# Attention's softmax denominators from GpSimd's sums of three probability chunks, both parts in one accumulation, and two passes over the early weights moved to ScalarE

## The chip, the cores and the metric

The kernel runs on one core of a Trainium2 chip. Times are device microseconds of one execution. TensorE (PE) multiplies, VectorE (DVE) and ScalarE (ACT) read its results, GpSimd (POOL) works on SBUF only, and SyncE (SP) issues most DMAs. Engines run their own instruction lists in order and meet at semaphores.

## The reference, cut to what matters

A cross-attention with two softmaxes (496 context rows, and 16 "dca" rows with their own keys and values) is followed by a mixture-of-experts layer. Only the attention matters here: for each of 4 x 16 = 64 heads (HD = 32, 512 queries),

```python
def _attn(q, k, v):
    s = jnp.einsum('bhqd,bhkd->bhqk', q, k) * SCALE
    p = jax.nn.softmax(s, axis=-1)
    return jnp.einsum('bhqk,bhkd->bhqd', p, v)
ctx = _attn(qT, k, v)                      # 496 main keys
ctx_dca = _attn(qT, k_dca, v_dca)          # 16 dca keys
ctx = ctx + DCA_WEIGHT * ctx_dca
return ctx @ Wo + bo
```

## The kernel before, in words

The program runs in stages: projections, attention (`attend`), output projection with routing, and the experts in two passes. The change is in `attend`, apart from a small constant table.

Attention walks over 64 heads with a software pipeline. A step `u` of the loop has two slots (`p` = 0 and 1). In step `u` PE makes the scores of head `u` in the layout queries x keys (`scores`, tile `a_psS`, two matmuls in each slot); DVE takes the negated row maxima from them (L866 over the 496 main keys, L867 over the 16 dca keys). The maxima are turned by small matmuls (`max_rows`, `a_psM`, in slot 0 only), ACT copies them as two more rows behind the queries (L822), and for head `u - 2` PE makes the scores again, transposed and with the maximum subtracted (`scores_t`, `a_psT`, one chunk of 128 keys in each matmul, four chunks to a head). ACT exponentiates each chunk into the tiles P0 to P3 (`p_t`, L807); chunk 3 holds the last main keys and the dca keys.

Four heads make a group, and there are 16 groups. With a lag of six steps, the P chunks of a group are multiplied in pieces that PE takes one or two at a time in the eight slots `h` = 0 to 7 of four steps (`chunk`). A piece (`four`) is four matmuls, one per head, each into its own 32 partitions; in float32 the trace shows it as eight. There were ten pieces to a group: four for the main denominators (P0 to P3 against columns of ones, `a_psD`), four for the values (`a_psO`), one for the dca values (`a_psOd`) and one for the dca denominators (`a_psD` again). The order in every slot is: T (an `a_psT` matmul), two S (`a_psS`), T, then the slot's piece or pieces, and M (the four `a_psM` matmuls) where `p` is 0. `a_psS` is one pair of banks: the S of a slot wait until DVE has read those of the slot before. `a_psT` is two banks: a T waits for the exponential two before it.

DVE turns and inverts the denominators between its reductions (L830, L833, L836 for the main part, L846, L849, L853 for dca) and multiplies (L841, L856). POOL adds both parts (`o_sum`, L790), ACT rounds the sum to float16 (the "hi" half, L813), and POOL subtracts that to get the "lo" half (L794).

Beside this, 12 half matrices of expert weights are prepared during attention, one for each four steps: SP loads one into `a_raw` once the one before is split, and POOL makes its float16 half (L167), scales it in place (L172, with a tiny L171 ahead) and subtracts (L175).

Of the kernel before, what the change touches and what calls it, by code (L numbers as in the profile page):

```python
# [82 lines left out]
def build(nc, t, out, upto=99, dbg=None):  # L83
# [17 lines left out]
    with ctx:  # L101
# [57 lines left out]
        def split_half(pool, raw, loaded, arrived, k, half, m, n, piece):  # L159
# [32 lines left out]
def project(nc, t, sem, g_):  # L192
# [51 lines left out]
    with ExitStack() as ps:  # L244
# [80 lines left out]
        def _(pool):  # L325
# [12 lines left out]
            pool.memset(ones[:, 0, :], 1.0).then_inc(s["masks"], 1)  # L338
# [152 lines left out]
        def _(dve):  # L491
# [118 lines left out]
            dve.tensor_copy(ones[:, 1, :], m_main[:, :].broadcast_to([P, HD]))  # L610
            dve.tensor_copy(ones[:, 2, :], m_dca[:, :].broadcast_to([P, HD]))
# [85 lines left out]
def attend(nc, t, sem, g_):  # L697
# [7 lines left out]
    RING = (6, 7, 7, 8)  # L705
# [9 lines left out]
    d_t = sb("d_t", [P, S], F32)  # L715
    d_rec = sb("d_rec", [P, S // HD, 1], F32)
# [4 lines left out]
    names = """sel max m_mm mrow s_mm t_mm exp d_mm v_mm dca_mm d_seen dd_seen d_rec dd_rec rec_main rec_dca o_main o_dca o_sum o_hi o_lo"""  # L721
# [4 lines left out]
    with ExitStack() as ps:  # L726
# [45 lines left out]
        def _(pool):  # L772
# [11 lines left out]

            for u in range(LAST):
                gr, h = group(u, 0)
                if there(gr - 1) and h == 4:
                    pool.wait_ge(s["o_main"], gr)
                    pool.wait_ge(s["o_dca"], gr)
                    pool.tensor_tensor(o_sum[:, :], o_sum[:, :], r_dca[:, :], ALU.add).then_inc(s["o_sum"], 1)  # L790
                if there(gr - 1) and h == 6:
# [4 lines left out]
                if n is not None and j < 3:  # L796
                    m, k, half = early[n]
                    g_["split_half"](pool, raw[:, :, :], raw_ld, n + 1, k, half, m, n, j)

        @block.scalar  # L800
        def _(act):
            def exps(w, k):

                act.wait_ge(s["t_mm"], TB * w + k + 1)
                if w >= RING[k]:
                    act.wait_ge(s["v_mm"], TB * ((w - RING[k]) // G) + k + 1)
                act.activation(probs(w, k), psT[:, k % 2], ACT.Exp, scale=SCALE / (QS * QS)).then_inc(s["exp"], 1)  # L807
# [7 lines left out]
            for u in range(LAST):  # L815
                for p in range(2):
# [6 lines left out]
                    hi_part(*group(u, p))  # L823

        @block.vector
        def _(dve):
            def main_part(gr, h):
                if there(gr) and h == 4:
                    dve.wait_ge(s["d_mm"], gr + 1)
                    dve.transpose(d_t[:, :], psD[:, :]).then_inc(s["d_seen"], 1)  # L830
                if there(gr) and h == 5:
                    dve.wait_ge(s["d_seen"], gr + 1)
                    dve.reciprocal(d_rec[:, :, :], d_t[:, :].rearrange("p (a o) -> p a o", o=HD)[:, :, 0:1]).then_inc(s["d_rec"], 1)  # L833
                if there(gr) and h == 6:
# [955 lines left out]
```

## Time and profile before

| | |
|---|---|
| time, median of 3 runs (lowest to highest) | 1215.59 us (1213.75 to 1219.01) |
| the profiled execution's own time | 1215.54 us |
| its span | 1213.4 us |
| PE busy over the span | 1050.7 us, 87% |
| DVE, ACT, POOL busy | 631.5, 491.9, 558.6 us |
| `p_t` exponentials on ACT (L807) | 256 of 595 ns |
| maxima on DVE (L866) | 128 of 1194 ns |
| matmuls into `a_psD`, `a_psO` (L900) | 640 of 607 ns, 512 of 601 ns |

Busy time counts the matmul records with their overlaps merged; since matmuls are pipelined, the distance between the starts of two of them tells what one costs, not its duration. Attention lies between about 190 and 512 us of the span.

### The profile page before, as it was taken

How to read it: one execution, taken by the hardware profiler on the slowest of the kernel's cores; microseconds unless marked ns; L12 is line 12 of the kernel's file. 1: busy time of each engine (PE TensorE's matmuls, PEld its weight loads, DVE VectorE, ACT ScalarE, POOL GpSimd, SP SyncE). 2: the span in 40 equal slices, each digit the busy share in tenths (PEclk: the TensorE clock that was granted, in tenths of full speed). 3: DMA queues.
4: the chain of work that ended last, by engine and by line, in shares of the span. 5: the costliest groups of instructions: out<-in, count | busy, mean ns of one | idle time of the engine just before them, and what ended most of it. 6: DMA issues, size and time to landing. Idle time of an engine off the chain costs nothing. (4 is left out here: it accounts for less than half of the span.)

```text
span 1213.4 us, 18924 instructions
## 1 busy us (share of the span) xinstructions
PE 1050.7 (87%) x5825; PEld 478.9 (39%) x5826; DVE 631.5 (52%) x1123; ACT 491.9 (41%) x886; POOL 558.6 (46%) x505
## 2 busy tenths in 40 slices
PE   2789955999999999689439999999999999967896
PEld 1445431222222222145315545445545455523453
DVE  6777744677777777445543333233333322215644
ACT  2466553566666666323213333333333333312231
POOL 1365551143434421232337799898999800032111
PEclk9889985899999999889759999999999999989899
DMA  6144451222122211045136434333434311146244
GB/s 233 40 116 127 135 143 52 58 77 76 61 80 62 76 62 42 19 160 180 72 119 245 165 124 137 121 121 121 138 122 137 104 52 52 35 146 228 87 122 139
DMA packets 88074, 133.02 MB, mean 110 GB/s; under 512 B 7992, under 2 KB 46904, under 8 KB 88016
## 3 DMA queue, kind: packets, MB, share of 16 engines
q1 hardware_dynamic: 75040, 90.55, 23.5%
q0 software_dynamic: 11648, 40.38, 9.8%
q10 hardware_dynamic: 1328, 1.36, 0.4%
q8 instruction: 32, 0.52, 0.2%
q14 instruction: 26, 0.21, 0.1%
HBM read 85.60 MB, written 46.66 MB: 109 GB/s over the span
## 5 line engine op out<-in xcount | busy, mean ns | idle before, releaser
L866 DVE TENSOR_REDUCE nm<-a_psS 128x2 bf16<-128x992 f32 x128 | 152.8, 1194 | 83.9 <-PE a_psS L877 83.9
L807 ACT ACTIVATE p_t<-a_psT 128x512 f32<-128x512 f32 x256 | 145.6, 595 | 62.9 <-PE a_psT L893 59.0
L1706 PE MATMUL e_psU<-w_exp,e_xT 128*128 (+1 forms) x528 | 130.8, 384 | 11.4 <-issue 8.0
L1706 PE MATMUL e_psY<-w_exp,e_gT 128*128 (+1 forms) x528 | 128.1, 379 | 2.7 <-issue 1.7
L1706 PE MATMUL e_psG<-w_exp,e_uT 128*128 (+1 forms) x528 | 128.4, 379 | 2.2 <-DVE e_uT L1658 2.2
L893 PE MATMUL a_psT<-q_stk,k_stk 98*128 98x512 f16 x256 | 101.6, 402 | 0.4 <-ACT p_t L807 0.4
L877 PE MATMUL a_psS<-k_stk,q_stk 96*128 96x512 f16 x256 | 82.3, 405 | 21.9 <-DMA k_stk<-k_dram 14.5
L1687 DVE TENSOR_TENSOR e_g<-e_g,e_u 128x512 f32<-128x512 f32 x44 | 51.6, 1172 | 91.6 <-ACT e_g L1623 91.6
L175 POOL TENSOR_TENSOR w_exp<-e_raw,w_exp 128x1024 f32 (+1 forms) x42 | 90.8, 2161 | 6.0 <-POOL e_raw L172 4.5
L1658 DVE TENSOR_TENSOR e_gT<-e_psGT,e_gT 128x512 f16<-128x512 f32 x44 | 30.4, 692 | 108.0 <-ACT e_gT L1596 108.0
L900 PE MATMUL a_psD<-p_t,ones 128*32 128x512 f32 x640 | 85.1, 607 | 0.0
L167 POOL TENSOR_TENSOR w_exp<-e_raw,ws_tile 128x1024 f32 (+1 forms) x42 | 80.6, 1920 | 4.3 <-DMA e_raw<-in_L_ffn_Wup_dram 3.5
L1706 PEld LDWEIGHTS e_psU<-w_exp,e_xT 128*128 128x128 f16 x528 | 49.2, 99 | 84.1 <-issue 31.7
L1603 ACT ACTIVATE e_u<-e_psU 128x512 f32<-128x512 f32 x44 | 26.3, 597 | 119.1 <-PE e_psU L1706 119.1
L1706 PEld LDWEIGHTS e_psG<-w_exp,e_uT 128*128 128x128 f16 x528 | 50.6, 98 | 55.2 <-DVE e_uT L1658 2.5
L1706 PEld LDWEIGHTS e_psY<-w_exp,e_gT 128*128 128x128 f16 x528 | 50.7, 98 | 48.3 <-issue 5.2
L790 POOL TENSOR_TENSOR o_sum<-o_sum,r_dca 128x512 f32<-128x512 f32 x16 | 20.4, 1275 | 106.2 <-DVE r_dca L856 106.2
L900 PE MATMUL a_psO<-p_t,v_all 128*32 128x512 f32 x512 | 67.4, 601 | 0.0
L1623 ACT ACTIVATE e_g<-e_psG 128x512 f32<-128x512 f32 x44 | 26.3, 597 | 93.5 <-PE e_psG L1706 93.5
L822 ACT ACTIVATE q_stk<-a_psM 2x512 f16<-2x512 f32 x64 | 37.4, 585 | 65.7 <-PE a_psM L884 65.6
L167 POOL TENSOR_TENSOR w_exp<-a_raw,ws_tile 128x1024 f16<-128x1024 f32 x12 | 22.7, 1893 | 87.2 <-DMA a_raw<-in_L_ffn_Wsu_dram 45.9
L1658 DVE TENSOR_TENSOR e_xT<-e_psX,e_xT 128x512 f16<-128x512 f32 x44 | 30.4, 692 | 52.7 <-ACT e_xT L1596 52.7
(315 smaller groups left out, 1875.1 us busy)
## 6 DMA issues: line engine op xcount, KB each, us to landing
e_x<-xs_dram SPq DMA_DIRECT2D x38, 256.0 KB, 2.8
ys_dram<-e_y SPq DMA_DIRECT2D x38, 256.0 KB, 2.0
q_dram<-q_st SPq DMA_DIRECT2D x24, 256.0 KB, 2.8
k_dram<-k_st SPq DMA_DIRECT2D x24, 256.0 KB, 3.6
q_stk<-q_dram SPq DMA_DIRECT2D x64, 96.0 KB
k_stk<-k_dram SPq DMA_DIRECT2D x64, 96.0 KB
e_raw<-in_L_ffn_Wup_dram POOLq DMA_DIRECT2D x12, 512.0 KB, 4.2
e_raw<-in_L_ffn_Wgate_dram POOLq DMA_DIRECT2D x12, 512.0 KB, 4.2
```

The costliest lines, as they stand in the source:

```text
L167: pool.tensor_tensor(hi, w, ws, ALU.mult).then_inc(w_scaled, 1)
L175: pool.tensor_tensor(lo, w, hi, ALU.subtract).then_inc(split_done, 1)
L807: act.activation(probs(w, k), psT[:, k % 2], ACT.Exp, scale=SCALE / (QS * QS)).then_inc(s["exp"], 1)
L822: act.activation(q_stk[K3:KR, (u - 1) % SLOTS, :], psM[0:2, :], ACT.Copy, scale=1.0 / QS).then_inc(s["mrow"], 1)
L866: dve.tensor_reduce(pair[:, :, 0:1].rearrange("p q o -> p (q o)"), psS[:, :, 0:NMAIN], AX.X, ALU.max, negate=True)
L877: ins = pe.matmul(psS[:, i], q_stk[0:K3, u % SLOTS, q * P:(q + 1) * P], k_stk[0:K3, u % SLOTS, :], start=True, stop=True)
L893: pe.matmul(psT[:, k % 2], k_stk[0:KR, w % SLOTS, k * P:(k + 1) * P], q_stk[0:KR, w % SLOTS, :], start=True, stop=True).then_inc(s["t_mm"], 1)
L900: ins = pe.matmul(dst[j * HD:(j + 1) * HD, :], stationary(n), probs(n, k), start=first, stop=last, tile_position=(0, j * HD))
L1603: act.activation(u[:, j], psU[:, :], ACT.Copy, scale=1.0 / WS).then_inc(s["u_r"], 1)
L1658: return dve.tensor_tensor(pair[:, 1], src[:, :].rearrange("p (k n) -> p k n", n=P), pair[:, 0], ALU.subtract)
L1687: dve.tensor_tensor(g[:, :], g[:, :], u[:, j], ALU.mult).then_inc(s["g_r"], 1)
L1706: ins = pe.matmul(dst[:, :], stationary, moving, start=(k == 0 and chunks[0] == 0), stop=(k == len(terms) - 1 and chunks[-1] == KD - 1))
```

## The change

- The main denominators use POOL's sum of P0, P1 and P2 of each head (`p_sums`, a ring of six tiles `p_sum`), so two pieces are left for them: the sums against ones, and P3 against ones masked to the main keys.
- The denominator matrix has 32 columns of which the first half belongs to the main part and the second half to dca; P3 against it gives both, so the dca denominators need no piece of their own. A group has seven pieces. Slot 7 has none.
- DVE turns the denominators once, inverts two columns of each block, and spreads each of them. The dca spread and the main product stand together in slot 7, the dca product in slot 0 of the next group.
- ACT makes the float16 half and the scale pass of the early weights; POOL keeps the subtraction. The hi half of the attention output moves on ACT from `h` 4 to `h` 3; on POOL the sum moves from `h` 4 to `h` 2 and the lo half from 6 to 4.
- The rings of P chunks are smaller (5, 5, 6, 7 tiles for 6, 7, 7, 8).

PE around slots 2 to 5 of a group: ahead of a slot's piece stand T, S, S, T. `a_psD` are denominators, `a_psO` values; `p_t_2080` to `p_t_2083` are P0 to P3 before. Before:

```order
L900 MATMUL a_psD<-p_t_2082,ones 32x512 x4
L884 MATMUL a_psM<-ident_b,nm 2x128 x4
L893 MATMUL a_psT<-q_stk,k_stk 128x512
L877 MATMUL a_psS<-k_stk,q_stk 128x512 x2
L893 MATMUL a_psT<-q_stk,k_stk 128x512
L900 MATMUL a_psD<-p_t_2083,ones 32x512 x4
L900 MATMUL a_psO<-p_t_2080,v_all 32x512 x4
L893 MATMUL a_psT<-q_stk,k_stk 128x512
```

And now (`p_t_2084` is P3, `p_sum` the sum of the three others):

```order
L931 MATMUL a_psD<-p_sum,ones 32x512 x4
L915 MATMUL a_psM<-ident_b,nm 2x128 x4
L924 MATMUL a_psT<-q_stk,k_stk 128x512
L908 MATMUL a_psS<-k_stk,q_stk 128x512 x2
L924 MATMUL a_psT<-q_stk,k_stk 128x512
L931 MATMUL a_psD<-p_t_2084,ones 32x512 x4
L924 MATMUL a_psT<-q_stk,k_stk 128x512
```

Slot 3 has lost its second piece; slot 6 has lost one in the same way, and slot 7 its only one.

POOL over one group before: the early weights' passes (L167 to L175) and two operations of the output.

```order
L790 TENSOR_TENSOR o_sum<-o_sum,r_dca 128x512
L167 TENSOR_TENSOR w_exp<-a_raw,ws_tile 128x1024
L794 TENSOR_TENSOR oT_all<-o_sum,oT_all 128x512
L171 TENSOR_TENSOR seen<-ws_tile 128x1
L172 TENSOR_SCALAR a_raw<-a_raw 128x1024
L175 TENSOR_TENSOR w_exp<-a_raw,w_exp 128x1024
```

And now, from the step with slots 0 and 1 on:

```order
L802 TENSOR_TENSOR p_sum<-p_t_2081,p_t_2082 128x512
L805 TENSOR_TENSOR p_sum<-p_sum,p_t_2083 128x512
L175 TENSOR_TENSOR w_exp<-a_raw,w_exp 128x1024
L802 TENSOR_TENSOR p_sum<-p_t_2081,p_t_2082 128x512
L805 TENSOR_TENSOR p_sum<-p_sum,p_t_2083 128x512
L814 TENSOR_TENSOR o_sum<-o_sum,r_dca 128x512
L802 TENSOR_TENSOR p_sum<-p_t_2081,p_t_2082 128x512
L805 TENSOR_TENSOR p_sum<-p_sum,p_t_2083 128x512
L818 TENSOR_TENSOR oT_all<-o_sum,oT_all 128x512
```

The sum of the output (L814) now stands behind both additions of a head's P chunks.

ACT at the hi half of the output, before:

```order
L807 ACTIVATE p_t_2081<-a_psT 128x512
L822 ACTIVATE q_stk<-a_psM 2x512
L813 ACTIVATE oT_all<-o_sum 128x512
L807 ACTIVATE p_t_2082<-a_psT 128x512
L807 ACTIVATE p_t_2083<-a_psT 128x512
```

And now:

```order
L850 ACTIVATE q_stk<-a_psM 2x512
L835 ACTIVATE p_t_2083<-a_psT 128x512
L835 ACTIVATE p_t_2084<-a_psT 128x512
L841 ACTIVATE oT_all<-o_sum 128x512
L835 ACTIVATE p_t_2081<-a_psT 128x512
L835 ACTIVATE p_t_2082<-a_psT 128x512
```

The hi half moved from the middle of a step to the end of the step before, between the exponentials of two heads.

The diff, cut to its core:

```diff
-    RING = (6, 7, 7, 8)
+    RING = (5, 5, 6, 7)
+    SUMS = 6
...
+        def scale_half(act, raw, loaded, arrived, k, half, m, n, piece):
+            hi = w_exp[:, k % E * 2 + half, m, 0, :, :]
+            if piece == 0:
+                act.wait_ge(loaded, 16 * arrived)
+                act.activation(hi, raw, ACT.Copy, scale=WS).then_inc(w_scaled, 1)
+            else:
+                act.wait_ge(w_scaled, 2 * n + 1)
+                act.activation(raw, raw, ACT.Copy, scale=WS).then_inc(w_scaled, 1)
...
+            def p_sums(w):
+                at_least(pool, s["sums_mm"], (w - SUMS) // G + 1)
+                t_ = p_sum[:, w % SUMS, :]
+                pool.wait_ge(s["exp"], TB * w + 2)
+                pool.tensor_tensor(t_, probs(w, 0), probs(w, 1), ALU.add).then_inc(s["sum_1"], 1)
+                pool.wait_ge(s["exp"], TB * w + 3)
+                pool.wait_ge(s["sum_1"], w + 1)
+                pool.tensor_tensor(t_, t_, probs(w, 2), ALU.add).then_inc(s["sum_2"], 1)
+
             for u in range(LAST):
                 gr, h = group(u, 0)
-                if there(gr - 1) and h == 4:
+                if head(u - 2):
+                    p_sums(u - 2)
+                if there(gr - 1) and h == 2:
                     pool.wait_ge(s["o_main"], gr)
                     pool.wait_ge(s["o_dca"], gr)
                     pool.tensor_tensor(o_sum[:, :], o_sum[:, :], r_dca[:, :], ALU.add).then_inc(s["o_sum"], 1)
...
             def hi_part(gr, h):
-                if there(gr - 1) and h == 4:
+                if there(gr - 1) and h == 3:
                     act.wait_ge(s["o_sum"], gr)
...
+                n, j = early_at(u)
+                if n is not None and j < 2:
+                    m, k, half = early[n]
+                    g_["scale_half"](act, raw[:, :, :], raw_ld, n + 1, k, half, m, n, j)
...
+                if there(gr) and h == 7:
+                    at_least(dve, s["o_sum"], gr)
+                    dve.transpose(blocks(r_dca[:, :]), spread(1)).then_inc(s["rec_dca"], 1)
+                    dve.wait_ge(s["v_mm"], TB * (gr + 1))
+                    dve.wait_ge(s["rec_main"], gr + 1)
+                    at_least(dve, s["o_lo"], gr)
+                    dve.tensor_tensor(o_sum[:, :], psO[:, :], r_main[:, :], ALU.mult).then_inc(s["o_main"], 1)
...
             def chunk(gr, h):
-                if h < TB:
-                    denominator(gr, h)
-                if TB - 1 <= h < 2 * TB - 2:
-                    values(gr, h - TB + 1)
-                if h == 2 * TB - 2:
+                if h in (0, 1):
+                    values(gr, h)
+                if h in (2, 3):
+                    if h == 3:
+                        pe.wait_ge(s["exp"], TB * (gr * G + G))
+                    denominators(gr, h == 3)
+                if h in (4, 5):
+                    values(gr, h - 2)
+                if h == 6:
                     dca(gr)
-                if h == 2 * TB - 1:
-                    values(gr, TB - 1)
```

## Rows read from the trace of the kernel before

**Rows 1.** Busy time by engine in one stretch of attention, with PE's granted clock.

```profile
340.00:380.00 40.00, 40.00 (x280) 11.57 (x273) 30.90 (x52) 25.22 (x45) 15.82 (x13) 1.00 0.23 73
```

**Rows 2.** Timeline of PE, slots 6, 7, 0 and 3: start, length, instruction.

```profile
364.17 0.59 PE L877 MATMUL a_psS<-k_stk,q_stk 96*128 96x512 f16 x2
...
364.91 1.07 PE L900 MATMUL a_psOd<-p_t,v_all 128*32 128x512 f32 x8
365.79 1.04 PE L900 MATMUL a_psD<-p_t,ones 128*32 128x512 f32 x8
366.65 0.39 PE L884 MATMUL a_psM<-ident_b,nm 128*2 128x128 bf16 x4
366.97 0.39 PE L893 MATMUL a_psT<-q_stk,k_stk 98*128 98x512 f16 x1
367.20 0.60 PE L877 MATMUL a_psS<-k_stk,q_stk 96*128 96x512 f16 x2
...
369.27 0.59 PE L877 MATMUL a_psS<-k_stk,q_stk 96*128 96x512 f16 x2
...
371.44 0.60 PE L877 MATMUL a_psS<-k_stk,q_stk 96*128 96x512 f16 x2
...
375.68 0.60 PE L877 MATMUL a_psS<-k_stk,q_stk 96*128 96x512 f16 x2
...
378.50 0.60 PE L877 MATMUL a_psS<-k_stk,q_stk 96*128 96x512 f16 x2
```

**Rows 3.** Timeline of DVE in slot 7 and at the start of slot 0.

```profile
367.83 1.19 DVE L866 TENSOR_REDUCE nm<-a_psS 128x2 bf16<-128x992 f32 x1 [0.21 <-PE a_psS L877]
368.94 0.18 DVE L867 TENSOR_REDUCE nm<-a_psS 128x2 bf16<-128x32 f32 x1
369.07 0.69 DVE L841 TENSOR_TENSOR o_sum<-a_psO,r_main 128x512 f32<-128x512 f32 x1
369.68 0.24 DVE L849 RECIPROCAL d_rec<-d_t 128x16 f32<-128x16 f32 x1
```

**Rows 4.** Timeline of ACT and POOL: maxima, both halves, exponentials.

```profile
361.98 0.58 ACT L822 ACTIVATE q_stk<-a_psM 2x512 f16<-2x512 f32 x1 [0.60 <-PE a_psM L884]
362.58 0.63 ACT L813 ACTIVATE oT_all<-o_sum 128x512 f16<-128x512 f32 x1
363.12 1.75 ACT L807 ACTIVATE p_t<-a_psT 128x512 f32<-128x512 f32 x3
...
363.29 1.16 POOL L794 TENSOR_TENSOR oT_all<-o_sum,oT_all 128x512 f16<-128x512 f32 x1 [0.38 <-ACT oT_all L813]
...
367.07 0.58 ACT L822 ACTIVATE q_stk<-a_psM 2x512 f16<-2x512 f32 x1 [1.46 <-PE a_psM L884]
```

**Rows 5.** Timeline near the end of attention: exponentials, and T waiting for one.

```profile
493.14 2.22 ACT L807 ACTIVATE p_t<-a_psT 128x512 f32<-128x512 f32 x4
...
493.86 0.79 PE L893 MATMUL a_psT<-q_stk,k_stk 98*128 98x512 f16 x2 [0.37 <-ACT p_t L807]
```

**Rows 6.** POOL's operations by line: duration in ns, min/median/max.

```profile
L790 POOL TENSOR_TENSOR o_sum<-o_sum,r_dca x16: 1260/1278/1281, 243.2 to 509.2; 128x512 f32<-128x512 f32 x16
...
L175 POOL TENSOR_TENSOR w_exp<-a_raw,w_exp x12: 2130/2132/2138, 233.5 to 440.4; 128x1024 f16<-128x1024 f32 x12
...
L175 POOL TENSOR_TENSOR w_exp<-e_raw,w_exp x42: 2122/2130/2605, 680.0 to 966.3; 128x1024 f32 x24, 128x1024 f16<-128x1024 f32 x18
```

**Rows 7.** Timeline: two of POOL's additions back to back, in the output stage.

```profile
516.72 2.48 POOL L1045 TENSOR_TENSOR o_xb<-o_x,bo 128x512 f32<-128x512 f32 x2 [4.41 <-DMA bo<-in_L_xattn_bo_dram]
```

**Rows 8.** Groups by line before attention: a pass over as many elements on ACT.

```profile
L478 ACT ACTIVATE wkv<-wkv_raw 128x1024 f16<-128x1024 f32 x2 | 2.1, 1057 | 0.1
```

**Rows 9.** DMA issues in attention: size, median us to landing.

```profile
a_raw<-in_L_ffn_Wgate_dram SPq DMA_DIRECT2D x2, 512.0 KB, 5.7
```

**Rows 10.** Timeline of PE: the one S that waited for its stack.

```profile
261.87 0.60 PE L877 MATMUL a_psS<-k_stk,q_stk 96*128 96x512 f16 x2 [0.68 <-DMA k_stk<-k_dram]
```

**Rows 11.** PE alone in a stretch of the experts: busy, clock, DMA share, GB/s.

```profile
1064.00:1068.00 4.00, 2.36 (x13) 1.00 0.16 59
```

More of the change, by code:

```diff
@@ L790, in _ @@
                     pool.tensor_tensor(o_sum[:, :], o_sum[:, :], r_dca[:, :], ALU.add).then_inc(s["o_sum"], 1)
-                if there(gr - 1) and h == 6:
+                if there(gr - 1) and h == 4:
                     b, c = divmod(gr - 1, KD)
@@ L795, in _ @@
                 n, j = early_at(u)
-                if n is not None and j < 3:
+                if n is not None and j == 2:
                     m, k, half = early[n]
-                    g_["split_half"](pool, raw[:, :, :], raw_ld, n + 1, k, half, m, n, j)
+                    g_["split_half"](pool, raw[:, :, :], raw_ld, n + 1, k, half, m, n, 2)
         @block.scalar
@@ L859, in _ @@
                 for p in range(2):
-                    main_part(*group(u, p))
-                    dca_part(*group(u, p))
+                    inverse(*group(u, p))
                     if head(u):
@@ L894, in scores_t, with four, denominators @@
                           start=True, stop=True).then_inc(s["t_mm"], 1)
-            def four(dst, stationary, gr, k, first, last):
+            def four(dst, stationary, gr, moving, first, last):
                 for j in range(G):
                     n = gr * G + j
-                    ins = pe.matmul(dst[j * HD:(j + 1) * HD, :], stationary(n), probs(n, k), start=first, stop=last, tile_position=(0, j * HD))
+                    ins = pe.matmul(dst[j * HD:(j + 1) * HD, :], stationary(n), moving(n), start=first, stop=last, tile_position=(0, j * HD))
                 return ins
-            def denominator(gr, k):
-                if k == 0:
-                    at_least(pe, s["dd_seen"], gr)
-                pe.wait_ge(s["exp"], TB * (gr * G + G - 1) + k + 1)
-                ins = four(psD, lambda n: ones[:, 1 if k == TB - 1 else 0, :], gr, k, k == 0, k == TB - 1)
-                if k == TB - 1:
-                    ins.then_inc(s["d_mm"], 1)
+            def denominators(gr, last):
+                if not last:
+                    at_least(pe, s["d_seen"], gr)
+                    pe.wait_ge(s["sum_2"], (gr + 1) * G)
+                    four(psD, lambda n: ones[:, 0, :], gr, lambda n: p_sum[:, n % SUMS, :], True, False).then_inc(s["sums_mm"], 1)
+                else:
+                    four(psD, lambda n: ones[:, 1, :], gr, lambda n: probs(n, TB - 1), False, True).then_inc(s["d_mm"], 1)
             def values(gr, k):
```

59 lines of the change are left out of this document (27 added, 32 removed).

## The prediction

> **What bounds the kernel now.** I read the busy time by stretches first. In 40 us of attention PE is busy all 40, at full granted clock, while DVE, ACT and POOL are busy 30.9, 25.2 and 15.8 [rows 1]. That says: PE's work sets the pace, and taking matmuls away pays. But busy PE is pipelined PE, so I read the timelines next, from one S to the next S, slot by slot. A piece costs 0.88 us (365.79 less 364.91), the piece starts 0.74 after S, and M 0.88 after the last piece [rows 2]. The slot without M and with one piece lasts 2.07 us (367.20 to 369.27), with M 2.17 (369.27 to 371.44), slot 3 with two pieces 2.82, slot 6 with two pieces 3.03 [rows 2]. Adding up a group: slots 0, 2, 4 at 2.17, slots 1, 5, 7 at 2.07, slots 3 and 6 at 2.82 and 3.03, which makes 18.57 us.
>
> The 2.07 is not PE's. DVE starts its reduction 0.63 after S (367.20, 367.83), L867 starts 1.11 later and lasts 0.18, and the next S starts 0.15 after that, at 369.27 [rows 2, 3]. So S, reduction, next S is a closed ring of 0.63 + 1.11 + 0.18 + 0.15 = 2.07. Slots with one piece and no M run at the ring's pace, slots with M run 0.10 above it, and only slots 3 and 6 are PE's by far. The real room on PE is thus not the 3 pieces x 0.88 = 2.64 a group.
>
> **The change, part by part.** *Pieces.* Slot 3 falls from 2.82 to the ring's 2.07 (-0.75), slot 6 from 3.03 to 2.17 (-0.86). Slot 7's piece goes too, but that slot was the ring's already: nothing.
>
> *DVE.* One turn and one inversion less, hidden between reductions. In slot 7, however, two operations of 512 columns now stand ahead of the reduction. L841 takes 0.61 to the next start (369.07, 369.68), and it starts 1.24 after its reduction [rows 3]; two in a row, a turn taken at 0.63 by its likeness, put the next reduction at 1.21 + 0.63 + 0.61 = 2.45 after the last one, where the ring has 2.07. I take +0.28 to +0.38, and 0.28 in the sum since slot 7 then lasts 2.35. A group without new waits comes to 4 x 2.17 + 3 x 2.07 + 2.35 = 17.24 us, 1.33 less than before.
>
> *ACT.* Each of the two passes costs 1.06 us for a half matrix [rows 8], one at the end of the step of slots 4-5, one after 6-7. There ACT is free from its last exponential to the first of the next step, about 0.9 us, and the exponential that gets pushed back by 0.2 to 1 us is needed by PE only 2 us later. Hidden; if the cover were gone, up to 2.1 us a group. The pass waits for a load: SP may issue it after POOL's L175, about 2.5 us past S of slot 2, it lands 5.7 us later [rows 9] at 8.2, and ACT asks at 9.6. Hidden with 1.4 us to spare; both times are mine, from the chain below.
>
> *POOL and the hi half: the step that gives the gain back.* Count from S of slot 2. ACT does a step's exponentials of chunks 2 and 3 behind the maxima copy: M stands at 0.74 + 0.88 = 1.62, the copy starts 0.42 after M (366.65, 367.07), and what follows it 0.60 after the copy's start (361.98, 362.58) [rows 2, 4], so chunk 2 starts at 2.64 and ends at 3.24. Behind that, in POOL's list, stand from the step of slots 0-1 a second addition and L175, and from the step of slots 2-3 both additions and o_sum. An addition of P chunks does not stand in the trace, but L790 is the same form: 1.28 us, and 1.21 from start to start when nothing stands between (2.48 less 1.27) [rows 6, 7]; the same overlap makes L175's 2.13 a 2.07. POOL starts 0.08 after the end of what it waits for (362.58 + 0.63, 363.29) [rows 4]. From S of slot 0: 3.24 + 0.08 = 3.32; second addition, 4.53; L175, 6.60; first addition and its own semaphore, + 1.28 + 0.08 = 7.96; second, 9.17; o_sum, + 1.28 = 10.45; less the 4.24 of two slots, o_sum ends 6.21 us after S of slot 2. The hi half on ACT waits for exactly that, from 3.8 on, in front of the next head's exponentials. With 0.08 it starts at 6.29, the exponential behind it at 6.83 (363.12 less 362.58 is 0.54 [rows 4]), ending at 7.43, and T starts 0.12 after the end of the exponential it waited for (493.14 + 0.60 = 493.74, T at 493.86 [rows 5]): 7.55. This T (chunk 2, ahead of slot 5's S) would stand 0.32 behind M (366.65, 366.97 [rows 2]), at 4.24 + 1.62 + 0.32 = 6.18. PE loses 1.37 us, once a group, and behind it everything follows. A group of this kind takes 17.24 + 1.37 = 18.61, against 18.57.
>
> POOL's bounds: below, 1.21 for every operation, which I nearly use; above, L175 once took 2.605 for a median of 2.130 in the expert stage [rows 6], 1.22 times. With every link at that rate the chain of 7.1 us (10.45 less 3.32) grows by 0.22 x 7.1 = 1.6 us. I take the low end, as all 16 of L790 lie within 1.26 to 1.28.
>
> By the Trainium skill (GPSIMD Engine Reference, sections 3.1 and 4.1) a two-input elementwise operation costs GpSimd about 2.6 cycles an element at 1.2 GHz and belongs on VectorE. By that figure an addition would be an estimated 1.11 us, the four of the chain 0.4 to 0.5 shorter, and the whole some 5 us faster than my sum; the trace has 1.28, and I go by the trace.
>
> **The sum.** Group 0 has no hi half before it: -1.33. Groups 1 to 12 hold a half matrix: 12 x +0.04 = +0.5. Group 13 has no L175 (its second addition starts at 3.32, o_sum ends at 5.81, the stall is 0.97): -0.36. In the tail (group 14 from slot 3, group 15 without heads) every piece is PE's own: five pieces less (-4.4), a turn, an inversion and a turn less in the chain at the very end (at 0.69, 0.24 and 0.69 [rows 3]: -1.6), one stall (+1.0), and the sums of the last head reach PE about 1.2 late: -3.8. Total -5.0 us. The profiled execution took 1215.54, which is also the median of the runs: 1210.5. All steps outside attention stay.
>
> **The rivals.**
>
> A, the hi half does not stall PE, or stalls it by half. For it: nothing in rows 1 shows ACT short of time, and T has two banks of slack. Against: the wait is written in front of the exponentials, and 1.37 is the remainder after that slack. The stalls add 12 x 1.37 + 0.97 + 1.0 = 18.4 in my sum; without them 1192, with half of them 1201.
>
> B, PE's count rules after all: 16 x 2.64 = 42 us less, 1173. For it: PE busy 40 of 40 [rows 1]. Against: the 2.07 ring [rows 2, 3].
>
> C, slower: POOL is the new bound. It goes from 40% busy to 4 x 2.55 + 1.28 + 1.16 + 2.13 = 14.8 of 18.6 us in a group, beside DVE. Each 0.1 us on its chain of five operations goes straight into every one of 12 groups; from 0.42 us (6% on each operation) the kernel is slower than before. At the upper bound, 1.6 x 12 = 19 more: 1229; halfway, 1220. A stack load that lands late adds to this: before, one S in slot 2 waited 0.68 for it [rows 10], with the lead that slot 4 now has too, but there the stall covers it.
>
> D, the new idle of PE (9% and more, in one stall) lowers its clock. The granted clock stayed full where PE was busy 2.36 of 4 us [rows 11]. If one 2.17 us slot a group ran at half clock: 12 x 2.2 = 26 more, 1237. The Trainium skill (TensorE: Matmul & The Clock Gate, Part 1) has idling bring the half clock back; the row speaks against it for gaps of this kind.
>
> E, the change makes no difference at all, the tail's gain lost in its own waits: 1215.
>
> **How the numbers follow.** Forecast 50% (own range 1205 to 1216, from 0.4 us a group either way), A 20%, B 5%, C 18%, D 2%, E 5%. About 0.5%, 6.1 us, is what a measurement of this kernel tells from no change, so faster means below 1209.5, slower above 1221.7. The forecast gives 0.18 to faster and 0.32 to same; A and B add 0.25 to faster; E 0.05 and the small sizes of C 0.03 to same; the rest, 0.17, is slower. The range leaves out B, D, the lowest tail of A and the upper end of C, 17% in all: 1191 to 1224.
>
> **What would show it.** In the profile after: slots 3 and 6 at 2.07 to 2.2 us; slot 7 at 2.35; o_sum on POOL ending 6.2 us after S of slot 2; ACT idle about 2.5 us ahead of the hi half with POOL's o_sum as the releaser, in groups 1 to 14; T in slot 5 waiting 1.3 us for an exponential; PE busy near 88% in stretches of attention at full clock. If ACT's idle there is short, A is right; if POOL's additions take over 1.35 us, C; if slot 3 is shorter than 2.07, my ring is wrong.

## The result and the profile after

The changed kernel takes 1206.8 us (1206.5 to 1207.7) where the kernel before takes 1216.9 in the same five rounds: ratio 0.9915, 95% interval 0.9896 to 0.9935. The forecast was 1210.5 in a range of 1191 to 1224. The interval lies clear of 1; the profiled executions, which the rest of this document compares, took 1215.54 and 1206.69.

The page after, first its busy line, then some of its groups of instructions (busy us, mean ns of one, then idle time just before them and what ended it):

```profile
PE 1007.1 (84%) x5441; PEld 466.9 (39%) x5442; DVE 618.8 (51%) x1091; ACT 509.3 (42%) x910; POOL 681.6 (57%) x598
...
L802 POOL TENSOR_TENSOR p_sum<-p_t,p_t 128x512 f32<-128x512 f32 x64 | 81.3, 1270 | 71.5 <-ACT p_t L835 71.5
L924 PE MATMUL a_psT<-q_stk,k_stk 98*128 98x512 f16 x256 | 101.9, 403 | 22.4 <-ACT p_t L835 22.3
...
L805 POOL TENSOR_TENSOR p_sum<-p_sum,p_t 128x512 f32<-128x512 f32 x64 | 81.2, 1269 | 17.5 <-ACT p_t L835 11.4
```

The additions take 1.27 us each, and about half of them (60 of 128) start when an exponential of ACT ends. T now waits 22.3 us in all for an exponential. The stretch of rows 1, after the change (busy us and instructions of PE, its weight loads, DVE, ACT and POOL, then PE's granted clock, the DMA share and GB/s):

```profile
340.00:380.00 40.00, 34.23 (x224) 10.21 (x223) 28.24 (x48) 29.31 (x51) 30.24 (x24) 1.00 0.22 71
```

PE is busy 34.2 of 40 us where it was busy all 40 [rows 1], at full granted clock still, and POOL nearly doubled. PE's idle time is what the change bought; the time from one S to the next tells how much of it became speed. PE's timeline over slots 6, 7 and 2 to 5 of the next group (answering to rows 2):

```profile
343.92 0.59 PE L908 MATMUL a_psS<-k_stk,q_stk 96*128 96x512 f16 x2
...
346.08 0.60 PE L908 MATMUL a_psS<-k_stk,q_stk 96*128 96x512 f16 x2
...
348.38 0.59 PE L908 MATMUL a_psS<-k_stk,q_stk 96*128 96x512 f16 x2 [0.69 <-DVE nm L898]
...
352.81 0.61 PE L908 MATMUL a_psS<-k_stk,q_stk 96*128 96x512 f16 x2
...
354.99 0.60 PE L908 MATMUL a_psS<-k_stk,q_stk 96*128 96x512 f16 x2
...
357.06 0.59 PE L908 MATMUL a_psS<-k_stk,q_stk 96*128 96x512 f16 x2
...
358.68 0.39 PE L915 MATMUL a_psM<-ident_b,nm 128*2 128x128 bf16 x4
360.14 0.39 PE L924 MATMUL a_psT<-q_stk,k_stk 98*128 98x512 f16 x1 [1.08 <-ACT p_t L835]
360.37 0.60 PE L908 MATMUL a_psS<-k_stk,q_stk 96*128 96x512 f16 x2
```

Slot 6 fell from 3.03 to 2.16 (343.92 to 346.08) and slot 3 from 2.82 to 2.07 (354.99 to 357.06). Slot 7 rose to 2.30, and what released it was DVE. And slot 4, which was 2.17, lasts 3.31 (357.06 to 360.37): T waits for an exponential. What the exponential waits for stands on POOL and ACT (answering to rows 4):

```profile
352.93 2.14 POOL L175 TENSOR_TENSOR w_exp<-a_raw,w_exp 128x1024 f16<-128x1024 f32 x1
355.01 1.28 POOL L802 TENSOR_TENSOR p_sum<-p_t,p_t 128x512 f32<-128x512 f32 x1
356.44 1.26 POOL L805 TENSOR_TENSOR p_sum<-p_sum,p_t 128x512 f32<-128x512 f32 x1
357.66 1.28 POOL L814 TENSOR_TENSOR o_sum<-o_sum,r_dca 128x512 f32<-128x512 f32 x1
```

```profile
358.97 0.63 ACT L841 ACTIVATE oT_all<-o_sum 128x512 f16<-128x512 f32 x1 [2.41 <-POOL o_sum L814]
359.51 1.07 ACT L835 ACTIVATE p_t<-a_psT 128x512 f32<-128x512 f32 x2
```

POOL works from L175 to o_sum with one gap of 0.15 us; ACT has been done since 356.56 and waits 2.41 us for the o_sum that ends at 358.94.

Counted over attention: groups 1 to 12 go from 224.2 to 222.8 us, eleven of them 18.51 to 18.53 now, where before ten were 18.57 to 18.66 and two longer. Of the 8.4 us by which the span got shorter (1213.4 to 1205.0), 2.9 lie between the first S and the last (299.6 to 296.6 us), 3.8 in the tail (24.8 to 21.0 us from the last S to the end of attention), 0.2 before the first S, and about 1.1 in the output stage, where the first twelve matmuls found a faster clock (granted 0.53 from 517.5 to 523 before, 0.68 from 510.7 to 515 after), as one row of before and one of after show:

```profile
517.52 5.30 PE L1125 MATMUL o_psY<-wo,oT_all 128*128 128x512 f16 x12 [10.89 <-DMA wr<-in_L_ffn_Wr_dram]
```

```profile
510.78 4.05 PE L1158 MATMUL o_psY<-wo,oT_all 128*128 128x512 f16 x12 [9.80 <-DMA wr<-in_L_ffn_Wr_dram]
```

The next twelve took 2.76 us in both kernels. The changed kernel, run again below, took 4.73 for the first twelve, and the other kernels, with idles of about 10 us there too, between 4.13 and 5.30. So that last us is a chance of PE's clock and not the work of the change; 0.4 is spread over the rest.

### The profile page after: what moved, and what is told of

The parts are those of the page before. It is cut to its first block and busy times, and to the rows that moved or that the text cites. A ratio compares the mean times of both kernels' runs of the same rounds, so it can differ in the third digit from the quotient of the medians.

```text
span 1205.0 us, 18414 instructions
## 1 busy us (share of the span) xinstructions
PE 1007.1 (84%) x5441; PEld 466.9 (39%) x5442; DVE 618.8 (51%) x1091; ACT 509.3 (42%) x910; POOL 681.6 (57%) x598
## 3 DMA queue, kind: packets, MB, share of 16 engines
q10 hardware_dynamic: 1328, 1.36, 0.4%
## 5 line engine op out<-in xcount | busy, mean ns | idle before, releaser
L897 DVE TENSOR_REDUCE nm<-a_psS 128x2 bf16<-128x992 f32 x128 | 152.6, 1192 | 105.2 <-PE a_psS L908 104.6
L835 ACT ACTIVATE p_t<-a_psT 128x512 f32<-128x512 f32 x256 | 142.9, 595 | 30.2 <-PE a_psT L924 26.3
L1739 PE MATMUL e_psU<-w_exp,e_xT 128*128 (+1 forms) x528 | 129.7, 382 | 12.2 <-issue 10.1
L802 POOL TENSOR_TENSOR p_sum<-p_t,p_t 128x512 f32<-128x512 f32 x64 | 81.3, 1270 | 71.5 <-ACT p_t L835 71.5
L924 PE MATMUL a_psT<-q_stk,k_stk 98*128 98x512 f16 x256 | 101.9, 403 | 22.4 <-ACT p_t L835 22.3
L175 POOL TENSOR_TENSOR w_exp<-e_raw,w_exp 128x1024 f32 (+1 forms) x42 | 91.2, 2171 | 6.0 <-POOL e_raw L172 4.5
L805 POOL TENSOR_TENSOR p_sum<-p_sum,p_t 128x512 f32<-128x512 f32 x64 | 81.2, 1269 | 17.5 <-ACT p_t L835 11.4
L167 POOL TENSOR_TENSOR w_exp<-e_raw,ws_tile 128x1024 f32 (+1 forms) x42 | 80.3, 1911 | 4.8 <-DMA e_raw<-in_L_ffn_Wup_dram 4.0
L1567 POOL DMA_INDIRECT s_ya<-ys_dram,slot x20 | 19.1, 956 | 80.6 <-DVE s_acc L1700 77.1
L924 PEld LDWEIGHTS a_psT<-q_stk,k_stk 98*128 98x128 f16 x256 | 25.0, 98 | 96.2 <-issue 42.0
```

The source lines that it names most:

```text
L167: pool.tensor_tensor(hi, w, ws, ALU.mult).then_inc(w_scaled, 1)
L802: pool.tensor_tensor(t_, probs(w, 0), probs(w, 1), ALU.add).then_inc(s["sum_1"], 1)
L805: pool.tensor_tensor(t_, t_, probs(w, 2), ALU.add).then_inc(s["sum_2"], 1)
L897: dve.tensor_reduce(pair[:, :, 0:1].rearrange("p q o -> p (q o)"), psS[:, :, 0:NMAIN], AX.X, ALU.max, negate=True)
L924: pe.matmul(psT[:, k % 2], k_stk[0:KR, w % SLOTS, k * P:(k + 1) * P], q_stk[0:KR, w % SLOTS, :], start=True, stop=True).then_inc(s["t_mm"], 1)
L1739: ins = pe.matmul(dst[:, :], stationary, moving, start=(k == 0 and chunks[0] == 0), stop=(k == len(terms) - 1 and chunks[-1] == KD - 1))
```

## The experiments

Eleven other kernels and the changed one once more, in three batches on three chips (the last four experiments below are the third batch). The chips of the second and third take 1263.3 and 1261.4 us for the kernel before, that of the first 1218.6, so times are compared by their ratio to the kernel before. For the changed kernel, traced on the first and the last, the difference lies in the experts (PE is busy 139 of the 180 us from 620 to 800 on the last chip at a clock of 0.89, and 171 at 0.99 on the first), and its slot times in attention agree to 0.02 us wherever nothing waits for a transfer. The lengths of slots and groups are S to S in the timelines of PE. A "stack" is a pair of buffers, `q_stk` and `k_stk`, that holds one head's queries and keys for S and T; SP loads it (96 KB each), there are four, and a raw load is the 512 KB that goes into `a_raw`.

**The hi half one slot later**, behind the maxima copy of the next step, where the kernel before had it. In `hi_part` on ScalarE:

```diff
-                if there(gr - 1) and h == 3:
+                if there(gr - 1) and h == 4:
```

> The changed kernel with one line different: ACT makes the hi half in slot 4, behind the maxima copy, as the kernel before did, not at the end of the step before. Theory 1 (the changed kernel loses 1.14 to 1.34 us a group because the hi half waits for POOL's o_sum in front of the next head's exponentials): o_sum ends 6.13 us after S of slot 2 and the copy ends there at about 6.9, so nothing waits; slot 4 falls from 3.4 to 2.17 us, a group from 18.52 to 17.24, the kernel by 12 x 1.28 + about 2 = 17 us, to about 1190 (ratio to before 0.978). Rival A (POOL's load as such sets the pace, and the wait only shows it): another wait for POOL takes its place, o_lo to DVE's product in slot 7 or the sums to PE, and a group stays above 18.3. Rival B (PE's own 2.64 us a group become free): group 15.9, 1168.

Measured: 1204.75 us, ratio 0.9904 (0.9868 to 0.994). ACT's wait for o_sum is gone from the groups, slot 4 is 2.17 or 2.18 in every one, and the last S comes 4.8 us earlier (479.7 for 484.4), where the theory had about 17 for the kernel. Slot 5 took the time: 2.9 to 3.5 in most groups.

```profile
342.73 0.61 PE L908 MATMUL a_psS<-k_stk,q_stk 96*128 96x512 f16 x2 [1.10 <-DMA k_stk<-k_dram]
```

The stall was real and of the size given, but behind it stood a second bound nearly as late: the stack load of slot 6. Groups 12 and 13, after the last raw load, fall to 17.3. In the whole time this ratio can't be told from the 0.9915 of the changed kernel; it is the traces that tell them apart.

**o_sum ahead of the sums of P chunks.** In POOL's list:

```diff
             for u in range(LAST):
                 gr, h = group(u, 0)
-                if head(u - 2):
-                    p_sums(u - 2)
                 if there(gr - 1) and h == 2:
                     ...
+                if head(u - 2):
+                    p_sums(u - 2)
```

> The changed kernel with two pieces of POOL's list swapped: in the step of slots 2 and 3 o_sum stands ahead of that step's two additions of P chunks. The hi half stays where the change put it. Theory 1: o_sum starts as soon as L175 is over, about 2.4 us after S of slot 2, and ends at 3.7; ACT's last exponential of the step ends at 3.8, so the hi half does not wait and a group takes 17.24 us, the kernel about 1190 (0.978). If POOL's whole load is the bound (14.8 us a group by durations), it stays near 18.5. The two cures take different instructions away from the wait, so if both work the wait between them was the cause.

Measured: 1204.18, ratio 0.989 (0.9859 to 0.9921): the same picture by another way, with the last S 5.0 us earlier. SP's issues (SPq) and PE here:

```profile
353.30 0.38 SPq L157 DMA_DIRECT2D a_raw<-in_L_ffn_Wgate_dram  x1
353.84 0.74 SPq L776 DMA_DIRECT2D q_stk<-q_dram  x1
354.62 0.69 SPq L776 DMA_DIRECT2D k_stk<-k_dram  x1
```

```profile
357.32 0.60 PE L908 MATMUL a_psS<-k_stk,q_stk 96*128 96x512 f16 x2
360.64 0.61 PE L908 MATMUL a_psS<-k_stk,q_stk 96*128 96x512 f16 x2 [1.19 <-DMA k_stk<-k_dram]
```

The raw load of 512 KB is issued just ahead of the stacks of 96 KB for the S at 360.64, and k_stk lands about 6.0 us after its issue. By the updates of the stacks' semaphores in the same trace, pairs with no raw load near them land in 4.4 to 4.9 us, and those with one 1.3 us ahead in 5.2 to 6.2.

**The same, with DVE's two products one slot apart.** In `inverse` on VectorE:

```diff
-                    dve.tensor_tensor(o_sum..., ALU.mult)      # at slot 7
                 if there(gr - 1) and h == 0:
+                    dve.tensor_tensor(o_sum..., ALU.mult)
+                if there(gr - 1) and h == 1:
                     dve.tensor_tensor(r_dca..., ALU.mult)
```

> The kernel with POOL's o_sum first, and DVE's two products spread again: the main product goes from slot 7 to slot 0 of the next group, the dca product from slot 0 to slot 1. Theory (slot 7 lasts 2.29 us, not 2.07, because two operations of 512 columns stand ahead of DVE's reduction): slot 7 falls to 2.07, a group by 0.22, the kernel by 14 x 0.22 = 3 us against the kernel with o_sum first alone. Rival: slot 7 is long because PE there waits for the exponential of chunk 2, and nothing changes; or PE's first value piece in slot 0 now waits for the main product and slot 0 grows by 0.2 or more.

Measured: 1202.59, ratio 0.9873 (0.9838 to 0.9908), in the whole time not told from the kernel before it in this list. Slot 7 falls from 2.29 to 2.07 in most groups, which confirms that term; slot 5 stays at 2.3 to 3.4. The last S comes only 0.5 us earlier than there, not 3: among others, group 1 took 19.5 us for 18.1. There PE waited 1.0 us for k_stk, and then the granted clock (third number from the end of the second row) fell to 0.50:

```profile
237.17 0.61 PE L909 MATMUL a_psS<-k_stk,q_stk 96*128 96x512 f16 x2 [1.01 <-DMA k_stk<-k_dram]
```

```profile
238.00:240.00 2.00, 2.00 (x12) 0.59 (x12) 1.70 (x3) 0.60 (x1) 1.23 (x1) 0.50 0.23 79
```

**The passes on ScalarE alone**, added to the kernel before; on POOL `split_half` keeps only its last piece, L175.

```diff
+                n, j = early_at(u)
+                if n is not None and j < 2:
+                    ... scale_half(act, raw, raw_ld, n + 1, k, half, m, n, j)
```

> The kernel before with one part of the change alone: ACT makes the float16 half and the scale pass of the early weights, POOL only the subtraction. Denominators, pieces and the hi half stay as before. Theory: two passes of 1.06 us in each four steps lie in ACT's idle time and hold up no T; groups stay at 18.6 us, the kernel within 2 us of before (0.998 to 1.002). Rival: the exponential behind a pass comes late and PE waits: up to 2.1 us a group, 25 us more (1.02).

Measured: 1216.99, ratio 0.9993 (0.998 to 1.0005). Groups stay at 18.57 to 18.63 but for the first and one of 20.02. On the kernel before, this part of the change is worth nothing either way; POOL had room there (15.8 of 40 us busy [rows 1]).

**A smaller raw load**, on top of o_sum first. Eleven of the twelve raw loads bring an eighth of their bytes, so this kernel leaves out most of those expert weights and its output is wrong; it is for timing only. ACT's second pass multiplies by 1 in it.

```diff
+            if part:                              # all but the first
+                raw, src = raw[:, :, 0:64], src[:, :, 0:64]
             eng.dma_start(raw, src).then_inc(loaded, 16)
```

> The kernel with o_sum first on POOL, with eleven of its twelve loads of early weights cut to an eighth of their bytes (64 of 512 columns) and ACT's second pass made with a factor of 1, so the expert weights it prepares are wrong; every instruction and wait is kept. In that kernel slot 5 lasts 2.45 to 3.64 us since the S of slot 6 waits for its stack, which SP issues right behind the 512 KB load. Theory 2 (the bytes of that load stand ahead of the stack in the DMA queue): slot 5 falls to 2.07, a group to 17.24 to 17.5, the kernel by 12 x 1.0 = 12 us against o_sum first, to about 1191. Rival (the stack is late because it is issued a slot later or takes 5 us anyhow): slot 5 stays above 2.8.

Measured: 1234.4 us, ratio 0.9769 (0.9734 to 0.9804). Slot 5 is 2.07 to 2.14 in all groups, and groups from the second on take 17.2 to 17.6. The same place as above, S of slots 5 and 6:

```profile
355.05 0.59 PE L910 MATMUL a_psS<-k_stk,q_stk 96*128 96x512 f16 x2
357.21 0.60 PE L910 MATMUL a_psS<-k_stk,q_stk 96*128 96x512 f16 x2
```

Same order, same issues, fewer bytes, and the stacks behind such a load land 4.5 to 4.8 us after their issue, as if there were none: what makes them late is the raw load's transfer. A few S of slot 4 still wait up to 0.35 us for a stack; four stacks leave little slack even so.

**L175 first in POOL's list**, so that the raw load goes out earlier.

```diff
+                n, j = early_at(u)
+                if n is not None and j == 2:
+                    ... split_half(...)          # L175
                 if there(gr - 1) and h == 2:
                     ...                          # o_sum
                 if head(u - 2):
                     p_sums(u - 2)
```

> The kernel with o_sum first on POOL, and in the step of slots 0 and 1 the early weights' subtraction also ahead of the additions of P chunks. It then ends about 2.4 us after S of slot 0 instead of 6.5, so that SP is not held and issues the 512 KB load behind the stack of slot 4 at S of slot 0 + 4.5, about 2.7 us ahead of the next stack, as in the kernel before. Theory 2: slot 5 falls to 2.07, a group to 17.24, the kernel to about 1190 (0.979). Rival (POOL's own load of 14.8 us a group comes out in a further wait, since additions of P chunks now start up to 1 us later): a group stays above 18, or PE waits for the sums in slot 2.

Measured: 1238.3 us, ratio 0.9805 (0.9775 to 0.9835). Slot 5 is back at 2.07 in most groups, but slot 3 is now 2.3 to 2.7, and groups take 17.4 to 18.5. The load goes out right behind a pair of stacks, and that pair is late:

```profile
346.25 0.69 SPq L776 DMA_DIRECT2D q_stk<-q_dram  x1
346.98 0.69 SPq L776 DMA_DIRECT2D k_stk<-k_dram  x1
347.72 0.46 SPq L157 DMA_DIRECT2D a_raw<-in_L_ffn_Wgate_dram  x1
```

```profile
352.29 0.60 PE L908 MATMUL a_psS<-k_stk,q_stk 96*128 96x512 f16 x2 [0.52 <-DMA k_stk<-k_dram]
```

**The same with DVE's products one slot apart**, by the edit of the third experiment.

> The same with DVE's two products in slots 0 and 1 of the next group in place of 7 and 0. Theory: slot 7 at 2.07 as in the run that had this alone, a group at 17.0, 3 us less than the kernel before it in this list: about 1187 (0.976). Rival: what was gained in slot 7 is lost in slot 0, where PE's first values wait for the product.

Measured: 1240.4 us, ratio 0.9823 (0.9795 to 0.9852). Slot 7 loses up to 0.2 and slot 3 gives part of it back; the last S is 2.8 us earlier, and in the whole time the two can't be told apart.

**Only the merged denominators**, without POOL's sums and ACT's passes: nine pieces a group instead of seven, early weights on POOL, the hi half and the rings of P chunks as before. DVE's two products stand one slot apart, as in the third experiment. Of a long diff, two lines:

```diff
-    d_t = sb("d_t", [P, S], F32)
-    d_rec = sb("d_rec", [P, S // HD, 1], F32)
+    d_rec = sb("d_rec", [P, S // HD, 2], F32)
```

> The kernel before with the other half of the change alone: main and dca denominators in one accumulation (P3 against the two-part matrix), so nine pieces to a group, one turn and one inversion; no sums on POOL, all passes over the early weights on POOL, the hi half in slot 4, rings as before, DVE's products in slots 0 and 1. Theory of the ring of 2.07 us: slot 6 falls from 3.03 to 2.17, slot 3 stays 2.82, a group takes 17.7 us; with 2.5 us less in the tail the kernel takes about 1201 (0.987 to 0.989), less than the whole change (0.9915). Rival B (PE's count): 0.88 a group, the same; the two differ in slot 7 only. Rival (the gain is lost in stack loads as in the runs before): a group stays near 18.5.

Measured: 1245.4 us, ratio 0.986 (0.9829 to 0.9891), groups of 17.7 to 18.0 but for the first and two that waited for a stack. S of slots 3, 4, 6 and 7 in one of them:

```profile
351.28 0.60 PE L887 MATMUL a_psS<-k_stk,q_stk 96*128 96x512 f16 x2
354.11 0.60 PE L887 MATMUL a_psS<-k_stk,q_stk 96*128 96x512 f16 x2
...
358.35 0.59 PE L887 MATMUL a_psS<-k_stk,q_stk 96*128 96x512 f16 x2
360.52 0.60 PE L887 MATMUL a_psS<-k_stk,q_stk 96*128 96x512 f16 x2
```

Slot 6 falls to 2.17, slot 3 stays at 2.83, and no S or T waits on POOL. With two pieces more than the full change this kernel is faster than it. Some 0.2 us a group of that is due to DVE's products, not to the pieces.

**The changed kernel again**, on the chip of the last batch.

> The changed kernel as it is, run beside the next three, so that they can be compared with it on one chip. All theories: groups of 18.5 us with a slot 4 of 3.3 to 3.5, ratio to before 0.991 as measured, within 0.004.

Measured: 1254.6 us, ratio 0.995 (0.9931 to 0.9968). That is above the 0.9915 of the first chip and above its interval, though attention is the same: slot 4 is 3.2 to 3.7 as there, the last S at 483.8 (484.4 there). So 6.7 us of gain here and 10.1 there; what lies outside attention makes the difference, and its cause stays open.

**A fifth stack slot**, on top of L175 first and the products apart.

```diff
-    SLOTS = G
+    SLOTS = G + 1
-    SUMS = 6
+    SUMS = 5
```

> The kernel of the experiment in which GpSimd splits early weights first (then o_sum, then the sums of P chunks) and VectorE's two products stand in slots 0 and 1 of the next group; now with five stack slots instead of four (paid for by five p_sum buffers instead of six), so that SP may issue each pair of stack loads a step, about 4.3 us, earlier. Theory (once the hi half's wait is gone, only the stack loads' lateness stands between the groups and the ring): no slot waits for DMA k_stk any more, all slots are 2.07 or 2.17, a group takes 8 slots of 2.12 = 17.0 us, the last S comes near 188 + 128 x 2.12 + 2 to 4 = 461 to 464, some 20 to 23 us ahead of the changed kernel's 484.4; ratio to before 0.970 to 0.976. Rival (the transfers themselves are slower than they are asked for, bandwidth and not the time of issue): slots 3 or 5 stay at 2.3 to 3 and a group at 17.4 to 17.9, ratio 0.980 to 0.983 as without the fifth slot.

Measured: 1232.2 us, ratio 0.9773 (0.975 to 0.9796), 22.4 us less than the changed kernel on that chip. Every group from 1 to 13 takes 16.95 or 16.96 us, every slot 2.07 or 2.17, the last S comes at 463.5, and no S of these groups waits for a stack. The stretch 340 to 380:

```profile
340.00:380.00 40.00, 38.23 (x256) 11.49 (x251) 31.51 (x52) 31.24 (x54) 35.07 (x27) 1.00 0.26 87
```

POOL is busy 35 of 40 us and holds nobody up in these groups; slot timings fitted, while the ratio expected (0.970 to 0.976) was a little too good. The transfers are as slow as before: stacks with a raw load 1.2 us ahead land 5.1 to 5.9 us after issue. Issued a step earlier they are in time all the same, so an earlier issue is enough.

**Maxima over half the keys**, on top of it.

```diff
-  dve.tensor_reduce(..., psS[:, :, 0:NMAIN], AX.X, ALU.max, negate=True)
+  dve.tensor_reduce(..., psS[:, :, 0:NMAIN // 2], AX.X, ALU.max, negate=True)
```

> The previous kernel with the main maxima taken over the first half of their keys (496 of 992 elements a partition; the softmax subtracts a smaller reference, which cancels), so that the reduction after each S takes about 0.65 us instead of 1.19. Theory (the ring S, reduction, S sets the slots without M at 2.07, as the prediction took it): these fall to what TensorE's own work takes, 1.97, and the slots with M stay at 2.17; a group 4 x 1.97 + 4 x 2.17 = 16.6 us, 0.4 less; time 5 to 6 us less than the previous kernel. Rival (the 2.07 is TensorE's own work or the exponentials): no slot changes, group 17.0, time the same within 1.5 us. Second rival (the ring also carries the slots with M): all slots fall by 0.1 or more, group 16.2 or less.

Measured: 1217.3 us, ratio 0.9648 (0.9632 to 0.9665), 15 less than the kernel it is built on. Reductions and S of PE:

```profile
355.98 0.68 DVE L898 TENSOR_REDUCE nm<-a_psS 128x2 bf16<-128x496 f32 x1 [1.14 <-PE a_psS L909]
```

```profile
357.32 0.60 PE L909 MATMUL a_psS<-k_stk,q_stk 96*128 96x512 f16 x2
359.49 0.60 PE L909 MATMUL a_psS<-k_stk,q_stk 96*128 96x512 f16 x2
361.04 0.59 PE L909 MATMUL a_psS<-k_stk,q_stk 96*128 96x512 f16 x2
```

Slots with one piece and no M fall to 1.97 (355.35 to 357.32), with M they stay at 2.17, as the ring theory has it. What the expectation left out is slot 7, which since the change has neither piece nor M: 1.55 (359.49 to 361.04). A group takes 16.15, not 16.6. The three slots 1, 3, 5 give 0.1 each and slot 7 gives 0.5; the six steps before the first piece, ring-bound too, give 4.5 more. It is no free gain: where a key left out lies far above all those looked at, the exponential can overflow.

**The raw load from ScalarE's queue**, on top of o_sum first: gone from SP's list, and in ScalarE's after the exponentials of slot 3:

```diff
+                    n, j = early_at(u + 1)
+                    if p == 1 and n is not None and j == 0:
+                        act.wait_ge(split_done, n + 1)
+                        ... load_half(act, raw, raw_ld, k, half, m)
```

> The kernel with o_sum ahead of the sums of P chunks on GpSimd, and the 512 KB loads of a_raw issued from ScalarE's queue (behind the exponentials of slot 3) instead of SP's. Theory (the stacks come late because they stand behind the raw load in SP's queue): each raw load now runs beside the stacks, PE's waits for DMA k_stk in slot 5 vanish, slot 5 is 2.07, groups 17.2 to 17.4 with slot 7 of 2.29; ratio to before 0.977 to 0.982. Rival (the 16 DMA engines are what is shared, whatever the queue): the stacks are as late as before, slot 5 stays at 2.4 to 3.6 and groups at 18.0 to 18.8, ratio 0.989. Second rival: the issue on ScalarE costs 0.5 us and more ahead of an exponential, and slot 4 or 5 shows it as a wait for p_t.

Measured: 1262.7 us, ratio 1.0002 (0.9983 to 1.002), so all of the gain is gone. Issues, the wait, and what follows it:

```profile
304.48 0.38 ACTq L157 DMA_DIRECT2D a_raw<-in_L_ffn_Wsg_dram  x1
```

```profile
304.51 0.69 SPq L776 DMA_DIRECT2D k_stk<-k_dram  x1
```

```profile
309.12 0.39 PE L924 MATMUL a_psT<-q_stk,k_stk 98*128 98x512 f16 x1
311.22 1.03 PE L908 MATMUL a_psS<-k_stk,q_stk 96*128 96x512 f16 x2 [1.71 <-DMA k_stk<-k_dram]
312.05 0.63 PE L924 MATMUL a_psT<-q_stk,k_stk 98*128 98x512 f16 x1
312.61 1.94 PE L931 MATMUL a_psOd<-p_t,v_all 128*32 128x512 f32 x8
```

With the load in another queue, issued at the same moment, k_stk lands even later, 5.9 to 6.8 us after issue. The raw load is itself slower in most cases, 4.7 to 5.5 us for 3.2 to 3.8, and ACT waits up to 1.0 us for it in its first pass, in front of the next exponentials. So standing behind it in the queue is not what makes a stack late: the two delay each other across queues as well. The first rival holds, and the cost was larger than either theory gave, for PE's clock fell: after the 1.7 us wait a piece takes 1.94 us for 1.06 and S 1.03 for 0.60. The windows say the same:

```profile
306.00:310.00 4.00, 3.51 (x26) 0.96 (x25) 3.29 (x6) 2.31 (x5) 3.77 (x4) 1.00 0.46 165
310.00:315.00 5.00, 3.78 (x16) 1.07 (x17) 2.48 (x4) 2.20 (x4) 2.19 (x2) 0.66 0.14 48
```

This happened in groups 3 to 6, whose slot 6 took 3.8 us instead of 2.17. Groups 2, 7 and 10 had as long a wait in slot 5 and kept the clock (1.00 in 270 to 276, 370 to 375 and 427 to 432); group 10:

```profile
428.95 0.60 PE L908 MATMUL a_psS<-k_stk,q_stk 96*128 96x512 f16 x2 [1.84 <-DMA k_stk<-k_dram]
```

## Why the prediction was right, and where its reasons fell short

**The ring.** Right: slot 3 fell to 2.07 and not to PE's 1.97, slot 6 to 2.16. Shortening the reduction frees exactly the slots that the prediction called the ring's, and leaves those with M. This is why 2.64 us a group of PE's work were worth 1.61 (0.75 + 0.86), and rival B's 1173 was never to be had.

**The sum, term by term.** Attention gave 6.7 us where the sum had 5.0: group 0 -0.9 for -1.33, groups 1 to 12 -1.5 for +0.5, group 13 -0.6 for -0.36, the tail -3.8 for -3.8. In group 0 slots 0 and 1 ran in part at half clock (granted 0.50 from 217 to 222), in both kernels, and slot 1 lasted 2.91 against 2.49. The measured gain is 8.9 us between the profiled executions and 10.1 between the medians, close to twice the forecast 5.0; 1.1 of it is the chance in the output stage. The mechanism held, and the groups were mis-sized by 2 us.

**DVE in slot 7.** +0.22 measured (2.29 against 2.07), +0.28 predicted; moving the products removed it. The +0.28 was a choice more than a sum: two products in a row come to 1.24 + 0.63 + 0.61 = 2.48 by its own rows (it wrote 1.21 and 2.45), 0.41 above the ring.

**The hi half.** Right in place and size. Its chain starts at S of slot 0, which stands at 348.38 above. From there o_sum ended at 10.56 (10.45 predicted), the hi half began at 10.59 (10.53), the exponential at 11.13 (11.07), T at 11.76 (11.79). POOL's second addition starts 1.41 to 1.43 after the first, not 1.36; ACT woke 0.03 us after POOL, not 0.08, and T came 0.63 after the exponential's start, not 0.72; these nearly cancel. Since the chain hangs on slot 0, slots 0 to 4 take 11.99 or 12.00 together in eleven of groups 1 to 12. The stall is 1.34 (1.37 forecast) where slots 1 and 3 run freely, and down to 1.1 where an S there came up to 0.2 late for its stack: the stall covers that. A group was 18.52, not 18.61, 0.06 of it from slot 7. That makes 1.1 us less than the sum had in twelve groups. Another 1.4 are what the groups of before exceeded 18.57 by, 1.0 of it in two that waited for a stack (19.33 and 18.79), and one group of 19.0 in the changed kernel takes 0.5 back.

**POOL's price.** 1.27 us an addition (1.26 to 1.29 over 144), 1.22 to 1.24 from start to start behind one that it doesn't depend on, as taken from the nearest rows, and the upper bound of 1.22 times did not occur. The prediction's estimate of 1.11, from the 2.6 cycles an element of the Trainium skill (GPSIMD Engine Reference, section 3.1), was too low. So rival C stays away; POOL is a bound only through the order of its list, as the five-slot kernel shows with POOL busy 88%.

**The tail.** -3.8 predicted, -3.8 measured, and only the total agrees. With o_sum first the tail is 2.0 us shorter still (18.95 for 20.95), so what POOL's order costs there is about 2.0 and not the +1.0 of the sum. The other terms, not measured one by one, must have given about 1.0 more than forecast: that the two cancel is luck.

**Rival A was priced wrongly, and that is the term to learn from.** It said that without the stall the kernel takes 1192, 18.4 us less than with it. The runs say about 1204 on that chip: two ways of removing the stall gave 0.9904 and 0.989. By the traces attention ended 6.2 and 7.1 us earlier than in the changed kernel (505.4, 499.2, 498.3). The sum "17.24 without waits" left out the stack loads. One sentence under C saw them, one S that waited 0.68 [rows 10], and dismissed them since the stall covered them. That was true of the changed kernel, and false of what the stall costs: with the stall gone, stacks are the next bound at 17.7 to 18.8 a group. A forecast by A would have been 12 us too low. The smaller load, the earlier issue and the fifth slot show it three ways.

**Rival D** had no part in the changed kernel, full clock from 222 to 470 us with PE busy 88%; it did come about with the load on ScalarE's queue, in four groups of the seven with waits of 1.6 us and more, and once in the third experiment.

**What the change was worth by parts.** Passes on ScalarE: nothing (0.9993). Merging, with DVE's products apart: 0.986 alone. All three parts: 0.995 on a like chip. So the sums on POOL cost more than they saved as placed; they were not run alone. What the traces show is that they lie in front of o_sum, L175 and thus the raw load. Where their order and the stack slots are mended, all three together reach 0.9773, the best kernel here that computes with all the maxima. How much of the last step belongs to the fifth slot and how much to five sum buffers wasn't separated, nor was merging alone tried with five stack slots.

## What to carry to other kernels

A stall's size is not what its removal brings: before pricing the kernel without it, list what else would be late by less than that stall, loads above all, by the time from issue to need. An engine's list in order is a chain: work that nobody needs soon, placed ahead of work that another engine waits for, makes that engine wait for both, and reordering or one more buffer can be worth more than the work that was saved. Find the ring of dependences before counting an engine's work, then test it by shortening one link.

## What the runs showed of the hardware

- A transfer of 512 KB delayed a 96 KB one that was in flight with it, in each order and queue tried. By the updates of the stacks' semaphores, k_stk landed 4.4 to 4.9 us after issue with no raw load near (o_sum first). It took 5.2 to 6.2 with one 1.3 us ahead (the same kernel), 4.9 to 5.4 with one 0.7 behind (before, and L175 first), and 5.9 to 6.8 with one at the same moment in another queue. With 64 KB in place of the 512, 1.3 us ahead, it took 4.5 to 4.8. The raw load itself landed in 3.2 to 3.8 us when issued ahead of the stacks (but for the first) and in 5.4 to 6.0 behind them.
- PE's granted clock stayed full (1.00 from 222 to 470) through the wait of 1.0 to 1.5 us in each of groups 1 to 12 of the changed kernel. With the load on ScalarE's queue it fell after a wait of 1.7 us (0.66 in 310 to 315, 1.00 in the 4 us before) in four groups but not in three others with such a wait, and in the kernel with DVE's products apart once after one of 1.0 us (0.50 from 238 to 240). What decides between them stays open; the length of the last wait alone does not.
- After idles of about 10 us the first twelve 128x512 matmuls of the output stage took 4.05 to 5.30 us, and in the changed kernel itself 4.05 in one execution and 4.73 in another; the next twelve took 2.76 in every run.
- Additions on POOL beside reductions, turns and products on DVE kept their 1.27 us also with POOL busy 88% and DVE 79% of the stretch (the kernel with five stack slots, 340 to 380).
